# Selective-scan block on one core: the scan's input u*B moved to TensorE, the readout over four blocks, the squares and a quarter of the weighing by C on VectorE

## The chip, the cores and the metric

The kernel runs on 1 core of one Trainium2 chip. The metric is the device time of one execution in microseconds. Times below come from 3 runs and from one more execution that the hardware profiler recorded.

## The reference, cut to what matters

x has 2 sequences of 2048 steps and 256 channels. A feed-forward block, the selective-scan block and the feed-forward block again are applied, each with its residual. The change is about the scan:

```python
dt = soft_clamp(softplus(xc @ W_dt.T + b_dt), 0.001, 0.1, 0.5)     # [2, 2048, 512]
Bp = xc @ W_B.T;  Cp = xc @ W_C.T                                  # [2, 2048, 16]
dA = exp(soft_clamp(dt[..., None] * A, -8.0, 8.0, 0.5))            # [2, 2048, 512, 16]
dB = dt[..., None] * Bp[:, :, None, :]
def step(h, inp):                                                  # h: [2, 512, 16]
    h = h * dA_t + dB_t * x_t[:, :, None]
    nrm = sqrt(sum(h * h, axis=(1, 2)))
    fac = minimum(20.0 / (nrm + 1e-08), 1.0)
    h = where(t % 10 == 0, h * fac, h)
    y = einsum('bdn,bn->bd', h, C_t) + D_param * x_t
    return h, y
```

Every tenth step the state of a sequence is rescaled by its norm over all 512 x 16 entries, so blocks of ten steps have to follow each other.

## The kernel before, in words

The kernel has three stages, each written out by hand as one instruction list per engine, with semaphores between them: pre_stage (first feed-forward block, projections, convolution, dt and u = dt*xc; 8 tiles of 256 steps), scan_stage and post_stage (output projection and second feed-forward block). Between stages the tensors go through DRAM.

In the scan stage the 512 channels are 4 groups (KE) of 128 partitions. A *unit* m is one block j = m // 2 of ten steps of one sequence b = m % 2: there are NB = 205 blocks and UNITS = 410 units. A unit holds 64 rows (4 groups x 16 states, NCH) of 11 columns (W): column 0 takes the state that is carried over, the other ten the steps. Per unit the engines do this (lines of the profile in brackets):

- ScalarE: two rows of tanh for a later chunk (L924, `tanhs`), the copy of a sum out of PSUM (L942, `copy_q`), the decays by exp (L952), the carry, which writes the rescaled last state of unit m - 2 into column 0 of unit m in PSUM (L960), and the squares of the last state with their sum per partition (L934, `squares`).
- VectorE: `inputs`, the product u*B of the unit after next, written to PSUM (L1031), and `scan`, the recurrence itself over 704 columns, decays from SBUF and inputs from PSUM (L1042). u lies in PSUM: TensorE copies six blocks of it there at a time with an identity product (L856, `move_u`); only the last half chunk is read from SBUF.
- TensorE: the sum over partitions of the squares (L850, `total`), the readout, which sums the weighted states over the 16 states n by accumulating identity products over a pair of blocks (L867), and `repeat`, one readout product done once more into a place that nothing reads (L877).
- POOL: `norm`, which clips the sum (L813) and takes its power -1/2 (L818), and `weigh`, the product of the 640 states with C into hc (L826). Its list is norm(m + 2), weigh(m), norm(m + 3), weigh(m + 1) and so on.
- SP issues the loads. C and B come as blocks broadcast over the partitions (`load_bc`), u as half chunks.

A float32 product on TensorE is two records in the trace. The squares of unit m + 2 wait for the scan of m, the sum for the squares, the copy for the sum, `norm` for the copy, the carry for `norm`, and the scan of m + 2 for the carry: the loop that passes from scan to scan of one sequence, with the other sequence in between.

```python
            scan(m)
            if m + B < UNITS:
                inputs(m + B)
```

Of the kernel before, what the change touches and what calls it, by code (L numbers as in the profile page):

```python
# [13 lines left out]
P = 128  # L14
B, L, D = 2, 2048, 256
E = 512
# [17 lines left out]
HALF = CT // 2  # L34
# [9 lines left out]
SECOND = 96 * 1024  # L44
# [4 lines left out]
    zT_ready yT_ready v_place""")  # L49


def pre_stage(nc, dram, w, areas, banks, sem):
# [28 lines left out]
    v_place = second.offset  # L81
    v = second.put("v", [P, KE, COLS])
    e = second.put("e", [P, KE, COLS])
# [13 lines left out]
    raw2 = e[:].rearrange("p a (c d) -> p (a c) d", d=D)  # L97
# [48 lines left out]
    def dt_u(dve, i):  # L146
# [3 lines left out]
        dve.tensor_scalar(dt[:], e[:], DT_HALF / SHARP, DT_MID, ALU.mult, ALU.add).then_inc(dt_ready, 1)  # L150
# [5 lines left out]
    def sync(sp, scan, post):  # L156
# [39 lines left out]
        sp.dma_start(dram["bc"][:, :, L:LP], zero[0:2 * N, 0:B, :]).then_inc(padded, 16)  # L196
        store_r(0)
        for i in range(TILES):
# [8 lines left out]
            if i >= 1:  # L207
                store_dt_u(sp, i - 1)
            if i < LAST:
                store_r(i + 1)  # L210
            if i == 3:
                post.load_params(sp)
                sp.wait_ge(padded, 48)
                scan.load_first(sp)
        store_bc(LAST)

    def gpsimd(pool):
# [42 lines left out]
    def tensor(pe):  # L260
# [24 lines left out]
        def down(i):  # L285
            if i >= 1:
                pe.wait_ge(yT_ready, KD * i)
            for d in range(KD):
# [58 lines left out]
        for i in range(TILES):  # L347
# [16 lines left out]
            project_dt(i, 1, KE)  # L364
        project_bc(LAST)

    def scalar(act, scan, post):
# [54 lines left out]
        def softplus(i, m0, m1):  # L422
            if i >= 1:
                act.wait_ge(th_ready, i)
# [4 lines left out]
        def tanh_v(i):  # L429
            act.wait_ge(ring_read, use["dt", i, KE - 1] + 1)  # L430
            if i >= 1:
                act.wait_ge(dt_ready, i)
            act.activation(e[:], v[:], ACT.Tanh, scale=SHARP / (DT_HALF + 1e-8),
# [30 lines left out]
        for i in range(TILES):  # L464
            copy_z(i)
            if i == LAST:
                scan.tanhs(act, 0, 8, 14)
            if i >= 1:
# [37 lines left out]
        scan.squares(act, 0)  # L506
        scan.squares(act, 1)
# [8 lines left out]
    def vector(dve, scan, post):  # L516
# [102 lines left out]
        dve.wait_ge(padded, 48)  # L619
        for i in range(TILES):  # L620
            if i + 2 < TILES:
                stats1(i + 2)
                apply1(i + 2)
            convolve(i)
# [10 lines left out]
            if i == 4:  # L635
                scan.decay_scale(dve)
                post.residual_steps(dve)
# [3 lines left out]
               t3_done, conv_steps, xc_ready, zT_ready, yT_ready, v_place)  # L641
# [4 lines left out]
PAIRS = -(-NB // 2)  # L646
NCH = KE * N
HB = CB // 2
HALVES = -(-NB // HB)
# [6 lines left out]
DRING = 6  # L656

Scan = namedtuple("Scan", """sync gpsimd tensor scalar vector load_first tanhs decay_rates decay_scale
    decay_ready y_out y_copied y_summed inp_ready squares copy_q""")
# [14 lines left out]

def scan_stage(nc, dram, w, areas, banks, sem, pre):

# [866 lines left out]
```

## Time and profile before

| what | us |
|---|---|
| median of 3 runs (lowest, highest) | 1652.79 (1650.85, 1653.66) |
| profiled execution, its own time | 1652.22 |
| its span, first to last instruction | 1650.4 |
| VectorE busy | 1387.6 (84%) |
| TensorE busy (products) | 1382.1 (84%) |
| ScalarE busy | 1268.5 (77%) |
| POOL busy | 978.3 (59%) |
| mean granted clock of TensorE | 0.991 |

The pre stage fills roughly the first 425 us, the scan 425 to 1440 us, the post stage the rest. Busy shares are of the whole span; a stage has its own. A duration in the timeline runs from an instruction's start to its end, and since neighbours on an engine overlap a little, the step from one start to the next can be shorter than the duration.

### The profile page before, as it was taken

What the parts mean: (1) busy time and instruction counts of PE and PEld (TensorE: products, weight loads), DVE (VectorE), ACT (ScalarE), POOL (GpSimd) and SP (SyncE); (2) the same over time, 40 slices, a digit from 0 to 9 for tenths busy, and PEclk for the clock granted to TensorE, in tenths of its full rate; (3) what the DMA queues carried; (4) which work ended last, traced back from release to release, by engine and by line L of the source; (5) the groups of instructions that cost most, each with busy time, mean ns of one, the idle gap of its engine ahead of it and who ended that gap; (6) DMA issues with size and microseconds to landing.
All of it is one profiled execution on the core that took longest, in us unless ns stands there. A gap on an engine that the chain in (4) does not pass through costs nothing.

```text
span 1650.4 us, 24684 instructions
## 1 busy us (share of the span) xinstructions
PE 1382.1 (84%) x7160; PEld 1055.6 (64%) x7160; DVE 1387.6 (84%) x1684; ACT 1268.5 (77%) x3354; POOL 978.3 (59%) x1318
## 2 busy tenths in 40 slices
PE   6999999999577787778777777777777877799998
PEld 5555555553366666666666666666666666677776
DVE  7757655645599999999999999999999999987885
ACT  4454455558899999999999999999999996433333
POOL 1302222112388888988888888888888888800000
PEclk9999999999799999999999999999999999999999
DMA  7223356224244333433433342434243235565430
GB/s 244 77 78 97 111 148 165 76 92 143 73 122 112 84 93 91 105 80 102 108 86 93 92 105 75 109 85 105 77 113 83 79 89 160 154 205 160 147 115 26
DMA packets 202694, 179.88 MB, mean 109 GB/s; under 512 B 82816, under 2 KB 175040, under 8 KB 202560
## 3 DMA queue, kind: packets, MB, share of 16 engines
q1 hardware_dynamic: 201616, 176.99, 38.7%
q8 instruction: 58, 0.95, 0.2%
q10 hardware_dynamic: 944, 1.31, 0.2%
q14 instruction: 76, 0.62, 0.1%
HBM read 125.26 MB, written 53.57 MB: 108 GB/s over the span
## 4 chain that ended last, share of the span: by engine, by line
DVE 44%; PE 29%; issue 17%; ACT 6%; POOL 3%; DMA 1%; DVEq 0%; ACTq 0%; SPq 0%; POOLq 0%
DVE h L1042 35%; PE banks L326 7%; PE banks L318 5%; PE banks L293 4%; ACT tb L924 3%; PE banks L1185 3%; PE banks L1206 3%; DVE cv L585 3%; PE banks L1216 2%; DVE banks L1031 2%; PE banks L333 2%; POOL hc L826 1%; PE banks L867 1%; ACT sc_sq L934 1%; PE banks L281 1%
## 5 line engine op out<-in xcount | busy, mean ns | idle before, releaser
L1042 DVE TENSOR_TENSOR_SCAN h<-decay,banks 128x704 f32<-128x704 f32 x410 | 660.2, 1610 | 9.7 <-ACT banks L960 9.2
L867 PE MATMUL banks<-hc,w_ident 128*128 128x160 f32 (+1 forms) x3296 | 611.9, 309 | 18.2 <-POOL hc L826 17.7
L826 POOL TENSOR_TENSOR hc<-h,bc 128x640 f32<-128x640 f32 x410 | 590.8, 1441 | 0.0
L867 PEld LDWEIGHTS banks<-hc,w_ident 128*128 128x128 f32 x3296 | 485.5, 191 | 38.8 <-POOL hc L826 29.9
L924 ACT ACTIVATE tb<-dtc,a 128x320 f32<-128x320 f32 (+1 forms) x832 | 448.8, 556 | 4.8 <-DVE x L552 4.8
L1031 DVE TENSOR_TENSOR banks<-banks,bc 128x640 f32<-128x640 f32 x408 | 339.6, 833 | 44.4 <-issue 14.5
L850 PE MATMUL banks<-sc_ss,sc_ones 128*128 128x1 f32 x820 | 156.0, 259 | 215.3 <-ACT sc_sq L934 207.5
L850 PEld LDWEIGHTS banks<-sc_ss,sc_ones 128*128 128x128 f32 x820 | 123.2, 189 | 307.4 <-ACT sc_sq L934 303.3
L952 ACT ACTIVATE decay<-tb 128x640 f32<-128x640 f32 x410 | 298.1, 728 | 0.4
L818 POOL TENSOR_TENSOR rc<-qs,w_mhalf 128x1 f32<-128x1 f32 x410 | 226.8, 553 | 61.7 <-POOL qs L813 1.3
L236 POOL TENSOR_TENSOR ln_rz<-ln_vz,w_mhalf 128x4 f32<-128x4 f32 x8 | 13.9, 1734 | 280.8 <-DVE ln_vz L558 280.8
L877 PE MATMUL banks<-hc,w_ident 128*128 128x160 f32 x800 | 174.2, 299 | 0.0
L960 ACT ACTIVATE banks<-h,rc 128x64 f32<-128x64 f32 x410 | 154.2, 376 | 21.3 <-POOL rc L818 21.3
L813 POOL TENSOR_SCALAR qs<-nq 128x1 f32<-128x1 f32 x410 | 79.5, 194 | 114.3 <-ACT nq L942 84.2
L877 PEld LDWEIGHTS banks<-hc,w_ident 128*128 128x128 f32 x800 | 130.6, 190 | 0.0
L934 ACT ACTIVATE sc_sq<-h 128x64 f32<-128x64 f32 x410 | 125.4, 306 | 5.5 <-DVE h L1042 4.7
L318 PE MATMUL banks<-zT,win 128*128 128x512 f32 x256 | 113.8, 598 | 6.8 <-ACT gf L383 5.8
L326 PE MATMUL banks<-xc,wdt 128*128 128x512 f32 x256 | 114.1, 600 | 3.1 <-ACT sg L420 3.1
L1172 POOL TENSOR_TENSOR q_ln_rs<-q_ln_ve,w_mhalf 128x4 f32<-128x4 f32 x8 | 10.9, 1366 | 167.3 <-DVE q_ln_ve L1443 167.3
L1273 ACT ACTIVATE q_gf<-banks,w_b,w_a 128x512 f32<-128x512 f32 x64 | 50.0, 781 | 69.4 <-PE banks L1206 65.6
L318 PEld LDWEIGHTS banks<-zT,win 128*128 128x128 f32 x256 | 47.4, 190 | 68.5 <-issue 59.9
L942 ACT ACTIVATE nq<-banks 128x1 f32<-128x1 f32 x410 | 68.8, 168 | 24.5 <-PE banks L850 22.3
(109 smaller groups left out, 1621.0 us busy)
## 6 DMA issues: line engine op xcount, KB each, us to landing
bc<-scratch_blk SPq DMA_DIRECT2D x205, 320.0 KB, 3.5
uc<-scratch_u SPq DMA_DIRECT2D x35, 240.0 KB, 4.5
scratch_xc<-xc SPq DMA_DIRECT2D x8, 1024.0 KB, 4.8
scratch_sg<-sg SPq DMA_DIRECT2D x8, 1024.0 KB, 5.9
scratch_dt<-dt SPq DMA_DIRECT2D x8, 1024.0 KB, 6.2
scratch_u<-u SPq DMA_DIRECT2D x8, 1024.0 KB, 6.9
q_ys<-scratch_y SPq DMA_DIRECT2D x8, 1024.0 KB, 6.0
q_xc<-scratch_xc SPq DMA_DIRECT2D x8, 1024.0 KB, 8.8
```

Source lines behind the costliest of these rows:

```text
L318: mm = pe.matmul(out, win[:, k, (m0 + m) * P:(m0 + m + 1) * P], zT[:, k, :], start=(k == 0), stop=(k == KD - 1))
L326: mm = pe.matmul(out, wdt[:, k, m * P:(m + 1) * P], xc[:, i % 2, k, :], start=(k == 0), stop=(k == KE - 1))
L818: pool.tensor_tensor(rc[:, b:b + 1], qs[:, b:b + 1], w.mhalf[:, 0:1], ALU.pow).then_inc(norm_ready, 1)
L826: pool.tensor_tensor(hc[:, pl % 2, :, j % 2 * S:(j % 2 + 1) * S] .rearrange("p (c b n) e -> p c b n e", c=KE, b=B)[:, :, b], state(m)[:, : ...
L850: pe.matmul(psQ[:, b:b + 1], ones[:], ss[:, b:b + 1], start=True, stop=True).then_inc(sum_ready, 1)
L867: mm = pe.matmul(psY[:, 0:KE * B * wide], w.ident[:], rhs, start=(n == 0), stop=(n == N - 1))
L877: pe.matmul(psQ[:, P:P + KE * B * 2 * S], w.ident[:], rhs, start=True, stop=True)
L924: act.activation(tanh_rows(c, r), dtc[:, c % 2, k * B:(k + 1) * B, 0:blocks_of(c) * S].rearrange("p b (k e) -> p k b e", e=S), ACT.Tanh, s ...
L952: act.activation(decay[:, m % DRING].rearrange("p (g i e) -> p g i e", g=DB, e=W)[:, :, :, 1:], tanh_block(j, b), ACT.Exp, scale=DTA_HALF ...
L960: act.activation(inp(m)[:, :, 0], state(m - B)[:, :, S], ACT.Copy, scale=rc[:, b:b + 1]).then_inc(carry_ready, 1)
L1031: dve.tensor_tensor(inp(m)[:, :, 1:].rearrange("p (c n) e -> p c n e", c=KE), u[:, b, :, o:o + S].unsqueeze(2).broadcast_to([P, KE, N, S]) ...
L1042: dve.tensor_tensor_scan(state(m).rearrange("p r e -> p (r e)"), decay[:, m % DRING], psI[m % B][:, 0:NCH * W], 0.0, ALU.mult, ALU.add).th ...
```

## The change

u*B is no longer made on VectorE. For every unit TensorE makes it as four float32r products (`inputs`, L988 of the changed kernel), one for each group of channels: the stationary operand holds u of the ten steps, each as high and low part and twice, in 40 rows; the moving operand holds B of these steps at the columns of their own step, 176 wide, zero elsewhere. The sum over the 40 rows gives u*B in float32r parts, and zero in column 0. The two operands are prepared in 32 *pieces* of 128 steps: load, transposes on TensorE (`turn_piece`), high part on ScalarE (`high_piece`), low part on VectorE (`low_piece`), the spreading of B by a mask on POOL (`mask_piece`), and the store to DRAM (`store_piece`). Pieces 0 and 1 are made within the pre stage, behind tiles 4 and 5; pieces 2 to 31 within the loop, one each 12 units. SP loads one unit's 40 rows per unit (`load_unit`), four units ahead.

The squares go from ScalarE to VectorE, behind the scan. The fourth group of channels of the weighing by C goes from POOL to VectorE (`weigh_last`), behind the squares. The readout takes four blocks at once (320 columns), a quad, in place of two (160 columns); `move_u` and `repeat` go. In the pre stage the buffer e goes (tanh works in place), and VectorE makes the masks once, behind tile 4.

```diff
         def weigh(m):
             j, b = m // B, m % B
-            pl = j // 2
+            pl = j // QB
+            if b == 0:
+                pool.wait_ge(bc_in[j % RING], 16 * (j // RING + 1))
             pool.wait_ge(h_ready, m + B + 1)
...
+            place, states, weights = weighed(m, 0, KE - 1)
+            pool.tensor_tensor(place, states, weights, ALU.mult).then_inc(hc_ready, 1)
...
+        def inputs(m):
+            pe.wait_ge(ub_in[m % URING], 16 * (m // URING + 1))
+            if m >= B:
+                pe.wait_ge(h_ready, m + 1)
+            for c in range(KE):
+                mm = pe.matmul(psI[m % B][:, c * N * W:(c + 1) * N * W], ub[m % URING][:, c * P:(c + 1) * P],
+                               ub[m % URING][:, E:], start=True, stop=True)
+            mm.then_inc(inp_ready, 1)
...
-                readout(p, quarter * 4, quarter * 4 + 3)
-                if m < UNITS - 6:
-                    repeat(p, m + B)
-                readout(p, quarter * 4 + 3, quarter * 4 + 4)
+                readout(p, part * each, (part + 1) * each)
...
-            if m + B < UNITS:
-                squares(act, m + B)
...
+        def squares(m):
+            b = m % B
+            dve.wait_ge(h_ready, m + 1)
             if m >= B:
-                dve.wait_ge(h_ready, m + 1)
-            dve.tensor_tensor(
-                inp(m)[:, :, 1:].rearrange("p (c n) e -> p c n e", c=KE),
-                u[:, b, :, o:o + S].unsqueeze(2).broadcast_to([P, KE, N, S]),
-                bc[j % RING][:, 0, b].unsqueeze(1).broadcast_to([P, KE, N, S]),
-                ALU.mult).then_inc(inp_ready, 1)
+                dve.wait_ge(sum_ready, m - B + 1)
+            last = state(m - B)[:, :, S]
+            dve.scalar_tensor_tensor(out=sq[:, b, :], in0=last, scalar=1.0, in1=last, op0=ALU.mult, op1=ALU.mult,
+                                     accum_out=ss[:, b:b + 1]).then_inc(sq_ready, 1)
...
+        def weigh_last(m):
...
+            place, states, weights = weighed(m, KE - 1, KE)
+            dve.wait_ge(h_ready, m + B + 1)
+            dve.tensor_tensor(place, states, weights, ALU.mult).then_inc(last_ready, 1)
...
         for m in range(UNITS):
             scan(m)
             if m + B < UNITS:
-                inputs(m + B)
+                squares(m + B)
+            weigh_last(m)
+            if m - 1 in pieces:
+                low_piece(dve, pieces[m - 1], psT)
...
+            if i in (4, 5):
+                scan.load_piece(sp, i - 4)
+            if i in (5, 6):
+                scan.store_piece(sp, i - 5)
```

`weighed(m, c0, c1)` gives the places in hc, the states in h and the values of C (tile bc) for the groups c0 to c1 of a unit. h, hc, bc and sc_sq lie in SBUF.

How the instructions stand on VectorE in the middle of the loop, before (h<-decay,banks is the scan, banks<-banks,bc the product u*B; banks are PSUM):

```order
L1042 SCALAR_TENSOR_TENSOR h<-decay,banks 128x704 [waits hc_ready,decay_ready,carry_ready]
L1031 TENSOR_TENSOR banks<-banks,bc_101 128x64x10 [waits h_ready]
L1042 SCALAR_TENSOR_TENSOR h<-decay,banks 128x704 [waits hc_ready,decay_ready,carry_ready]
L1031 TENSOR_TENSOR banks<-banks,bc_102 128x64x10 [waits h_ready,bc_in3]
L1042 SCALAR_TENSOR_TENSOR h<-decay,banks 128x704 [waits hc_ready,decay_ready,carry_ready]
```

and on VectorE in the changed kernel, at the same place, with one piece in it:

```order
L1158 SCALAR_TENSOR_TENSOR h<-decay,banks 128x704 [waits hc_ready,last_ready,decay_ready,carry_ready]
L1149 SCALAR_TENSOR_TENSOR sc_sq,sc_ss<-h 128x64 [waits sum_ready,h_ready]
L1170 TENSOR_TENSOR hc<-h,bc_97 128x16x10 [waits h_ready,bc_in1]
L1158 SCALAR_TENSOR_TENSOR h<-decay,banks 128x704 [waits hc_ready,last_ready,decay_ready,carry_ready]
L1149 SCALAR_TENSOR_TENSOR sc_sq,sc_ss<-h 128x64 [waits sum_ready,h_ready]
L1170 TENSOR_TENSOR hc<-h,bc_97 128x16x10 [waits h_ready]
L853 TENSOR_TENSOR turned<-banks,turned 128x528 [waits ut_hi]
```

Two short instructions with h as an input have taken the product's place. POOL in the changed kernel, with qs and rc the two operations of `norm`, and the same piece:

```order
L959 TENSOR_TENSOR hc<-h,bc_96 128x3x16x10 [waits h_ready]
L943 TENSOR_SCALAR qs<-nq 128x1 [waits q_copied]
L948 TENSOR_TENSOR rc<-qs,w_mhalf 128x1 [waits q_held,carry_ready]
L959 TENSOR_TENSOR hc<-h,bc_97 128x3x16x10 [waits h_ready,bc_in1]
L943 TENSOR_SCALAR qs<-nq 128x1 [waits q_copied]
L948 TENSOR_TENSOR rc<-qs,w_mhalf 128x1 [waits q_held,carry_ready]
L959 TENSOR_TENSOR hc<-h,bc_97 128x3x16x10 [waits h_ready]
L861 TENSOR_TENSOR spread<-turned,mask 128x352 [waits ub_out,ut_lo]
```

Its order is the old one; the weighing is three groups wide in place of four. On TensorE, before:

```order
L850 MATMUL banks<-sc_ss,sc_ones 128x1 [waits q_copied,sq_ready]
L867 MATMUL banks<-hc,w_ident 128x160 x3
L877 MATMUL banks<-hc,w_ident 128x160 [waits q_copied]
L867 MATMUL banks<-hc,w_ident 128x160
L850 MATMUL banks<-sc_ss,sc_ones 128x1 [waits q_copied,sq_ready]
```

and in the changed kernel:

```order
L981 MATMUL banks<-sc_ss,sc_ones 128x1 [waits q_copied,sq_ready]
L988 MATMUL banks<-ub_101 128x176 [waits h_ready,ub_in1]
L988 MATMUL banks<-ub_101 128x176 x3
L1001 MATMUL banks<-hc,w_ident 128x320 x2
L981 MATMUL banks<-sc_ss,sc_ones 128x1 [waits q_copied,sq_ready]
```

The sum still leads the unit; the four input products stand between it and the readout, which is two products of double width.

## Rows read from the trace of the kernel before

**Rows 1.** Stretches: start:end, us, PE PEld DVE ACT POOL busy (x), PEclk, DMA share, GB/s.

```profile
500.00:900.00 400.00, 316.41 (x2000) 271.59 (x2001) 386.87 (x329) 393.82 (x1193) 352.64 (x495) 1.00 0.38 96
900.00:1300.00 400.00, 316.56 (x2003) 271.50 (x2002) 386.83 (x330) 394.17 (x1193) 352.96 (x494) 1.00 0.37 93
```

**Rows 2.** Groups by line and form, VectorE, whole span: busy us, mean ns.

```profile
L1031 DVE TENSOR_TENSOR banks<-banks,bc 128x640 f32<-128x640 f32 x408 | 339.6, 833 | 44.4 <-issue 14.5 <-DVE h L1042 0.9
...
L585 DVE SCALAR_TENSOR_TENSOR cv<-xbuf,convw,cv 128x512 f32<-128x512 f32 x96 | 65.0, 747 | 0.0
...
L1053 DVE TENSOR_TENSOR h<-u,b 128x64 f32<-128x64 f32 x2 | 0.4, 276 | 0.0
```

**Rows 3.** Timeline of one unit, all engines: start us, us, instruction.

```profile
901.35 1.06 PE L867 MATMUL banks<-hc,w_ident 128*128 128x160 f32 x6
...
901.81 0.19 POOL L813 TENSOR_SCALAR qs<-nq 128x1 f32<-128x1 f32 x1
...
902.15 0.55 POOL L818 TENSOR_TENSOR rc<-qs,w_mhalf 128x1 f32<-128x1 f32 x1
...
902.66 1.45 POOL L826 TENSOR_TENSOR hc<-h,bc 128x640 f32<-128x640 f32 x1
902.71 0.83 DVE L1031 TENSOR_TENSOR banks<-banks,bc 128x640 f32<-128x640 f32 x1
902.73 0.38 ACT L960 ACTIVATE banks<-h,rc 128x64 f32<-128x64 f32 x1
...
903.25 0.18 ACT L934 ACTIVATION_READ_ACCUMULATOR sc_sq<-h 128x1 f32 x1
...
903.45 1.61 DVE L1042 TENSOR_TENSOR_SCAN h<-decay,banks 128x704 f32<-128x704 f32 x1
...
903.49 0.38 PE L850 MATMUL banks<-sc_ss,sc_ones 128*128 128x1 f32 x2 [0.54 <-ACT sc_sq L934]
...
903.91 0.17 ACT L942 ACTIVATE nq<-banks 128x1 f32<-128x1 f32 x1
...
904.20 0.19 POOL L813 TENSOR_SCALAR qs<-nq 128x1 f32<-128x1 f32 x1
```

**Rows 4.** Timeline, end of the loop, POOL and VectorE.

```profile
1433.81 1.44 POOL L826 TENSOR_TENSOR hc<-h,bc 128x640 f32<-128x640 f32 x1
...
1434.30 1.64 DVE L1031 TENSOR_TENSOR banks<-uc,bc 128x640 f32<-128x640 f32 x1
...
1435.34 0.64 POOL L813 TENSOR_SCALAR qs<-nq 128x1 f32<-128x1 f32 x1
...
1438.69 1.61 DVE L1042 TENSOR_TENSOR_SCAN h<-decay,banks 128x704 f32<-128x704 f32 x1
```

**Rows 5.** Timeline, 24 us earlier, POOL and VectorE.

```profile
1405.78 1.44 POOL L826 TENSOR_TENSOR hc<-h,bc 128x640 f32<-128x640 f32 x1
...
1406.99 0.79 DVE L1303 SCALAR_TENSOR_TENSOR q_ys<-q_xc,dpar,q_ys 128x512 f32<-128x512 f32 x1
```

**Rows 6.** Timeline of VectorE: scans of units 0, 10 and 392.

```profile
429.76 1.61 DVE L1042 TENSOR_TENSOR_SCAN h<-decay,banks 128x704 f32<-128x704 f32 x1
...
460.86 1.62 DVE L1042 TENSOR_TENSOR_SCAN h<-decay,banks 128x704 f32<-128x704 f32 x1 [0.35 <-ACT banks L960]
...
1392.60 1.61 DVE L1042 TENSOR_TENSOR_SCAN h<-decay,banks 128x704 f32<-128x704 f32 x1
```

**Rows 7.** Busy time by stretch, start of the loop; columns as in rows 1.

```profile
440.00:445.00 5.00, 0.59 (x2) 0.50 (x2) 3.94 (x5) 4.79 (x14) 3.94 (x6) 0.50 0.18 66
455.00:460.00 5.00, 3.48 (x24) 3.24 (x24) 4.40 (x4) 4.99 (x17) 3.67 (x7) 1.00 1.07 326
```

**Rows 8.** Timeline at the end of tile 4 of the pre stage: SP, TensorE.

```profile
278.75 0.51 SPq L137 DMA_DIRECT2D scratch_u<-u  x1
...
282.01 1.04 PE L311 MATMUL banks<-w_ident,zn 128*128 128x128 f32 x8
```

**Rows 9.** The page, DMA issues: KB each, median us from issue to landing.

```profile
uc<-scratch_u SPq DMA_DIRECT2D x35, 240.0 KB, 4.5
```

More of the change, by code:

```diff
@@ L258, in gpsimd, with tensor @@
                 norm2(i + 1)
-    def tensor(pe):
+            if i in (5, 6):
+                scan.mask_piece(pool, i - 5)
+    def tensor(pe, scan):
         def fill(what):
@@ L636, in vector @@
                 scan.decay_scale(dve)
+                scan.masks(dve)
                 post.residual_steps(dve)
@@ L656 @@
 DRING = 6
[L658 to L659 removed]
+URING = 4
+PIECES = B * L // P
+SPLITS = 4
+ROW = E + N * W
+Scan = namedtuple("Scan", """sync gpsimd tensor scalar vector load_first load_units tanhs decay_rates decay_scale masks
+    decay_ready y_out y_copied copy_q load_piece turn_piece high_piece low_piece mask_piece store_piece ut_lo""")
 def chunk_of(j):
@@ new lines, in store_piece @@
+    def store_piece(sp, k):
+        t, b = k // B * P, k % B
+        rows = dram["ub"][b, t:t + P].rearrange("t (r h) x -> t r h x", h=2)
+        sp.wait_ge(ut_lo, k + 1)
+        for r in range(2):
+            sp.dma_start(rows[:, r, :, 0:E], turned[:, :, 0:E].bitcast(F32)).then_inc(ub_out, 16)
+        sp.wait_ge(spread_done, k + 1)
+        for half in range(2):
+            sp.dma_start(rows[:, :, half, E:], spread[:].bitcast(F32).rearrange("p r n e -> p r (n e)")
+                         ).then_inc(ub_out, 16)
@@ L870, in readout @@
                 mm.then_inc(y_summed, 1)
-        def repeat(p, m):
-            pe.wait_ge(q_copied, m + 1)
-            rhs = hc[:, p % 2].rearrange("p (c n) t -> p c n t", n=N)[:, :, 0]
-            pe.matmul(psQ[:, P:P + KE * B * 2 * S], w.ident[:], rhs, start=True, stop=True)
+        pieces = {piece_unit(k): k for k in range(B, PIECES)}
+        each = N // (QB * B)
         pe.wait_ge(consts, 1)
+        pe.wait_ge(pre.zT_ready, KD * TILES)
+        pe.wait_ge(pre.yT_ready, KD * TILES)
+        pe.wait_ge(ut_lo, B)
+        inputs(0)
+        inputs(1)
         pe.wait_ge(pre.ring_read, len(pre.order))
-        total(0)
-        move_u(0)
-        total(1)
+        for m in range(B):
+            total(m)
         for m in range(UNITS):
@@ L988, in rows_at @@
             return c + 1, half
+        pieces = {piece_unit(k): k for k in range(B, PIECES)}
         for m in range(AHEAD):
@@ L1057, in vector @@
                 ALU.mult).then_inc(h_ready, 1)
+        for m in range(B):
+            squares(m)
         dve.wait_ge(zeroed, 1)
-        for m in range(B):
-            inputs(m)
         pre.dt_u(dve, TILES - 1)
+        dve.wait_ge(pre.ring_read, len(pre.order))
+        dve.wait_ge(pre.sg_out, 16 * TILES)
+        dve.wait_ge(pre.xc_out[0], 16 * TILES // 2)
+        dve.wait_ge(pre.u_ready, TILES)
+        pieces = {piece_unit(k): k for k in range(B, PIECES)}
         for m in range(UNITS):
@@ L1236, in tensor @@
         turn_xn(0)
[L1237 removed]
+        pe.wait_ge(scan.y_copied, QUADS)
         up(0, 0, 1)
@@ L1490, in _ @@
             def _(pe):
-                pre.tensor(pe)
+                pre.tensor(pe, scan)
                 scan.tensor(pe, post)
```

294 lines of the change are left out of this document (183 added, 111 removed).

## The prediction

> **What bounds the kernel now.** The busy table puts VectorE, TensorE and ScalarE all near 80% of the span, which says only that several engines are close. The stretches tell more [rows 1]: from 500 to 1300 us VectorE is busy for 97% and ScalarE for 98% of the time, and two VectorE operations are counted per unit (one batch's ten steps), so 659 operations in 800 us make 2.43 us a unit. The by-form groups and the timeline say what fills a unit: the scan takes 1.61 us and its successor starts some 1.7 us after it, and the product u*B takes 0.833 us with the next scan 0.74 us behind its start [rows 2, 3]. VectorE waits for nothing; 1.7 + 0.74 is the period.
>
> Beside it runs a loop that comes back every second unit: squares, the sum on TensorE, its copy on ScalarE, two small POOL operations (L813, L818), the carry, the scan. On POOL the weighing by C (L826) stands behind those two and is 1.44 us long [rows 3]. Today nothing on VectorE cares when the weighing runs.
>
> The third reading is the one that decides. At the end of the loop u comes from SBUF and not from PSUM, and the same product with two SBUF inputs takes 1.64 us where it took 0.83 [rows 4]. It starts at 1434.30, while POOL's weighing runs from 1433.81 to 1435.25, and ends at 1435.94, 0.69 us after the weighing. That is 640 elements at one per 1.04 ns and almost nothing else: VectorE got no element through while POOL's instruction ran. The scalar_tensor_tensor of 512 elements does the same: weighing over at 1407.22, product over at 1407.78, 0.56 us later [rows 5]. It works the other way as well: the short L813, 0.19 us elsewhere, starts at 1435.34 and lasts until 1435.98, just past the end of VectorE's product [rows 3, 4]. So on this chip a VectorE instruction with both inputs in SBUF and a POOL instruction that reads SBUF exclude each other for their whole length. The scan and the old product read one input from PSUM and aren't stretched: the one at 902.71 lies beside a weighing from 902.66 and takes 0.83 us, the mean of all 408 [rows 2, 3].
>
> **The change, part by part.**
>
> *Per unit on VectorE.* The product (0.74 us of step) goes. The squares come, 64 elements through scalar_tensor_tensor with both inputs the same SBUF column, and a quarter of the weighing, 160 elements of h by C, both in SBUF. From the 512-element row of 0.747 us, at 1.04 ns an element, the fixed part is 0.21 and the squares 0.28 us [rows 2]; the step to the next operation is about 0.09 less, as with the product. Writing the accumulator is not in the trace for VectorE. ScalarE's costs 0.09 us of step [rows 3]; bounds are 0 and the 0.18 us of its whole length, and I take 0.10. The quarter weighing is between 0.28 (64 elements) and 0.83 us (640 elements), by its size 0.32, step 0.24. Without any exclusion a unit would be 1.68 + 0.20 + 0.10 + 0.24 = 2.22 us, 0.22 under today's.
>
> The Trainium skill (VectorE: DVE Perf Modes, the section on the TRN2 errata) gives an fp32 tensor_tensor as element count plus 151 cycles at 0.96 GHz, which would make 64 elements 0.224 us. The row here shows 0.276 for 64 elements [rows 2], so the measured one is used; by the page that sum would be 2.17.
>
> *Per unit on POOL.* The weighing falls to 480 elements: 1441 x 3/4 = 1.08 us, or 1.13 if 0.19 us of it is fixed (the shortest POOL row). I take 1.08.
>
> *The order that follows.* POOL's queue is L813, L818, weighing; the first two wait for the squares of the same pass. I follow one pass from the moment the previous weighing frees SBUF: squares through 0.09 (64 elements and the 0.02 seen at 1434.30), accumulator 0.10, to TensorE 0.06 (903.43 to 903.49), TensorE to the copy 0.42, copy to L813 0.29, L813 to L818 0.34, L818 to the weighing 0.51, the weighing itself 1.08 [rows 3]. That makes 2.89 us. Meanwhile VectorE does squares 0.19, quarter weighing 0.25, scan 1.65 and comes to the next squares at 2.1. The weighing has been running since 1.81. So the squares wait 0.8 us, every unit, and what they wait for is itself started by the squares before: a closed ring of **2.89 us** a unit. The carry is in at 1.30 + 0.58 + 0.4 = 2.3, before its scan is wanted at 3.3, so it adds nothing. The wait is new; behind it on VectorE stand the quarter weighing and the scan, and TensorE, ScalarE and POOL wait in turn.
>
> *The other engines fit beneath it.* ScalarE loses squares and accumulator (0.30) of 2.43, leaving about 2.1. TensorE: the readout issues 4 records of 320 columns in place of 8 of 160, at 0.15 a 160-column record (six in 1.06 us, the last of which runs 0.3) [rows 3] 1.2 us at most; ten records become four, since the repeated products go too; four input products of 176 columns at no more than 0.15 each 0.6; the sum 0.24. That is 2.0, hidden under 2.89; without that cover it would still be under 2.22. Loads of C halve, the 410 loads of u and B rows stand on SP, four units ahead: nothing waits on them.
>
> *The 30 pieces within the loop* put five transposes on TensorE, 528 elements each on ScalarE and VectorE (0.69 us for 512 from PSUM, 0.62 of step) and 352 elements on POOL (0.8 us at the weighing's rate). VectorE has 0.8 us free and POOL about 0.9 between weighing and L813, so I count 0; if each cost its POOL time in full it would be 24 us.
>
> *Before the loop.* SP issues the store of u at 278.75 in tile 4, the piece load follows behind it and lands some 4.5 us after issue, at about 284; TensorE is at the place of the transposes at 282 [rows 8, 9] and TensorE is what runs through there. Two pieces, each 2 to 3 us of wait and 0.7 of transposing, and some of the masks' 5 us on VectorE that isn't hidden: +8 (0 to 15). The two products ahead of the first scan go: -1.5.
>
> *Sum.* The first ten units take 3.11 us each now (429.76 to 460.86), since ScalarE has extra rows to do; at 2.89 that is -2. From 460.86 to 1392.60 lie 382 units at 2.44 [rows 6]: 382 x 0.45 = +172. The last sixteen take 2.88 us already, with skip and gate between (1392.60 to 1438.69) [rows 4, 6]; their two-SBUF operations will meet POOL more often: +2. Together -1.5 - 2 + 172 + 2 + 8 = +178. The profiled execution took 1652.2 us (span 1650.4 and 1.8 around it), the median of the runs is 1652.8, the same within 0.04%. 1652.2 + 178 = **1830 us**.
>
> **The rivals.**
>
> *Squares and weighing miss each other (faster).* The ring closes only because the weighing starts (1.81) before the scan ends (2.1): 0.3 us decides. If the squares, having one tensor as both inputs, took only one SBUF read, or such small instructions slipped in, VectorE would set 2.22 us: 382 x -0.22 = -84, the pieces then cost VectorE's 0.62 each, +19, before the loop +8, start and end -7: **1588 us**. Against it: both directions of the exclusion stand in the trace for tensor_tensor and for scalar_tensor_tensor. Also, squares ahead of the weighing don't help much: the quarter weighing right behind would then be the one shut out, with the scan behind it. For it: no row has an instruction this short, nor twice the same input. The Trainium skill (SBUF — State Buffer, Who interferes with whom) has the rule that speaks against this change: VectorE instructions with two SBUF inputs contend with POOL instructions that read SBUF, and the one that starts second is blocked fully. By that rule the squares are no exception; the trace agrees where it can be read (0.95 us of blocking at 1434.30). Chance 0.16.
>
> *They queue without the chain adding to it.* If POOL's work and VectorE's two short ones stood end to end, with no wait for the sum in between, a unit would be 0.34 + 0.51 + 1.08 + 0.10 (from the weighing's end to the next L813) + 0.19 + 0.25 = 2.47: 1671 us; orders that change from unit to unit lie between 2.47 and 2.89, to 1760 or so. It needs the weighing to be late often. 0.09, of which 0.03 ends within 0.2% of no change.
>
> *TensorE's clock falls.* The repeated products go, and TensorE's columns per unit with them. The granted clock stood at 0.50 (1.2 GHz) while TensorE did one sum per 3 us, and at 1.00 (2.4 GHz) from 455 on with ten records in 2.8 us [rows 7]; afterwards there are 4 x 320 + 4 x 176 columns in 2.89 us, more than 10 x 160 in 2.8. At half clock the readout alone is 2.3 us and the unit about 3.5: +405, **2060 us**. The Trainium skill (TensorE: Matmul & The Clock Gate, "A second HAM failure mode") reports a kernel in which brief idle spells between groups of products let the clock swing; no row here shows that inside the loop. 0.03.
>
> **How the numbers follow.** Forecast 0.72, missing each other 0.16, partly queued 0.09, clock 0.03. High end: weighing 1.13, accumulator 0.19 give 3.03 a unit, +225, and pieces at their full 24 with 8 before the loop: 1910. Low end: 1690, which takes in most of the partly queued orders and leaves out the fast case. Of no change this kernel's measurement can tell about 0.2%. Faster 0.16, same 0.03, slower 0.81.
>
> **What would show it.** Right: scans 2.89 us apart; the squares' row with a mean near 0.95 us where 0.28 is their own length, each ending just behind a weighing; the quarter weighing unstretched at 0.32; the weighing at 1.08; ScalarE's and TensorE's idle time on the squares' chain; clock 1.00. Wrong: squares at 0.3 us while the weighing runs (first rival), or scan steps over 3.2 with the clock at 0.50 (third).

## The result, and the profile after

The changed kernel takes 1830.87 us (median of 4 runs, 1828.37 to 1831.7) where the kernel before takes 1652.32 in the same comparison: ratio 1.1078, 95% interval 1.1059 to 1.1097. The forecast was 1830, with 1690 to 1910 as its range. The profiled execution has a span of 1826.5 us, 176.1 more than before.

Stretches of the loop, in the columns of [rows 1]:

```profile
500.00:900.00 400.00, 295.30 (x1456) 199.89 (x1455) 392.96 (x575) 299.85 (x731) 265.81 (x433) 0.98 0.48 134
900.00:1300.00 400.00, 299.57 (x1467) 203.83 (x1468) 392.70 (x576) 300.23 (x733) 265.51 (x434) 0.97 0.47 132
```

VectorE counts as busy for 98% of the time, TensorE, ScalarE and POOL for less than before. Someone with only this view would say that VectorE got too much work. The groups of the page say otherwise:

```profile
L1158 DVE TENSOR_TENSOR_SCAN h<-decay,banks 128x704 f32<-128x704 f32 x410 | 659.3, 1608 | 10.4 <-ACT banks L1084 7.4
...
L959 POOL TENSOR_TENSOR hc<-h,bc 128x480 f32<-128x480 f32 x410 | 461.4, 1125 | 1.0 <-DVE h L1158 0.6
...
L981 PE MATMUL banks<-sc_ss,sc_ones 128*128 128x1 f32 x820 | 158.4, 262 | 309.0 <-DVE sc_sq L1149 306.5
...
L1149 DVE SCALAR_TENSOR_TENSOR sc_sq<-h 128x64 f32<-128x64 f32 x410 | 368.0, 898 | 14.2
...
L943 POOL TENSOR_SCALAR qs<-nq 128x1 f32<-128x1 f32 x410 | 78.5, 191 | 375.7 <-ACT nq L1066 373.1
...
L1170 DVE TENSOR_TENSOR hc<-h,bc 128x160 f32<-128x160 f32 x410 | 152.5, 372 | 3.1 <-issue 1.8
```

64 elements of squares take 898 ns on average, while 160 elements of the quarter weighing take 372. The profile counts the time for which an instruction is blocked as busy time; it shows in the mean of one, set against its size. The idle time of TensorE (306.5 us) and POOL (373.1 us) stands on the chain that the squares start.

One unit in the timeline (start, us, instruction), against [rows 3]:

```profile
1000.31 0.17 ACT L1066 ACTIVATE nq<-banks 128x1 f32<-128x1 f32 x1 [0.80 <-PE banks L981]
...
1000.57 0.19 POOL L943 TENSOR_SCALAR qs<-nq 128x1 f32<-128x1 f32 x1 [0.87 <-ACT nq L1066]
...
1000.90 0.55 POOL L948 TENSOR_TENSOR rc<-qs,w_mhalf 128x1 f32<-128x1 f32 x1
1001.42 1.12 POOL L959 TENSOR_TENSOR hc<-h,bc 128x480 f32<-128x480 f32 x1
...
1001.63 1.03 DVE L1149 SCALAR_TENSOR_TENSOR sc_sq<-h 128x64 f32<-128x64 f32 x1
...
1002.60 0.08 DVE L1149 DVE_READ_ACCUMULATOR sc_sq<-h 128x1 f32 x1
1002.60 0.32 DVE L1170 TENSOR_TENSOR hc<-h,bc 128x160 f32<-128x160 f32 x1
...
1002.73 0.38 PE L981 MATMUL banks<-sc_ss,sc_ones 128*128 128x1 f32 x2 [0.83 <-DVE sc_sq L1149]
1002.84 1.61 DVE L1158 TENSOR_TENSOR_SCAN h<-decay,banks 128x704 f32<-128x704 f32 x1
...
1003.15 0.17 ACT L1066 ACTIVATE nq<-banks 128x1 f32<-128x1 f32 x1 [0.80 <-PE banks L981]
```

The squares start 0.21 us behind the weighing's start and end 0.12 us after its end at 1002.54. So it is in 322 units: where squares start within a weighing and last over 0.6 us, they end 0.11 to 0.14 us behind it. The ring comes round in 2.84 us (1000.31 to 1003.15): squares 0.12 behind the weighing, sum 0.07, copy 0.42, qs 0.26, rc 0.33, weighing 0.52, its length 1.12.

Where the 176 us lie, by the starts of scans (of after here, of before in [rows 6] and the last scan at 1440.20):

| stretch | before | after | difference | forecast |
|---|---|---|---|---|
| to the first scan | 429.8 | 442.6 | +12.8 | +6.5 |
| first ten units | 31.1 | 30.2 | -0.9 | -2 |
| 382 units in the middle | 931.7 | 1090.1 | +158.3 | +172 |
| the last 17 steps | 47.6 | 48.95 | +1.4 | +2 |
| behind the last scan's start | 210.2 | 214.7 | +4.5 | 0 |

```profile
442.57 1.62 DVE L1158 TENSOR_TENSOR_SCAN h<-decay,banks 128x704 f32<-128x704 f32 x1 [2.88 <-ACT decay L1076]
...
1611.81 1.62 DVE L1158 TENSOR_TENSOR_SCAN h<-decay,banks 128x704 f32<-128x704 f32 x1
```

### The profile page after: what moved, and what is told of

Its sections match the earlier page's. It is cut to its first block, busy times and chain, and to the rows that moved or that the text cites. A ratio compares the mean times of both kernels' runs of the same rounds, so it can differ in the third digit from the quotient of the medians.

```text
span 1826.5 us, 25399 instructions
## 1 busy us (share of the span) xinstructions
PE 1472.9 (81%) x6460; PEld 976.7 (53%) x6460; DVE 1565.1 (86%) x2553; ACT 1159.3 (63%) x2515; POOL 871.8 (48%) x1350
## 4 chain that ended last, share of the span: by engine, by line
PE 35%; POOL 35%; DVE 12%; issue 8%; ACT 6%; DMA 2%; POOLq 1%; SPq 0%; DVEq 0%; ACTq 0%
POOL hc L959 21%; POOL rc L948 10%; PE banks L981 8%; PE banks L330 4%; PE banks L338 4%; POOL qs L943 4%; ACT nq L1066 3%; PE banks L305 3%; PE banks L1322 3%; PE banks L1001 3%; PE banks L1343 3%; DVE cv L597 3%; DVE h L1158 2%; DVE sc_sq L1149 2%; PE banks L1353 2%
## 5 line engine op out<-in xcount | busy, mean ns | idle before, releaser
L1001 PE MATMUL banks<-hc,w_ident 128*128 128x320 f32 (+1 forms) x1664 | 537.3, 448 | 0.8 <-ACT yc L1095 0.6
L959 POOL TENSOR_TENSOR hc<-h,bc 128x480 f32<-128x480 f32 x410 | 461.4, 1125 | 1.0 <-DVE h L1158 0.6
L981 PE MATMUL banks<-sc_ss,sc_ones 128*128 128x1 f32 x820 | 158.4, 262 | 309.0 <-DVE sc_sq L1149 306.5
L981 PEld LDWEIGHTS banks<-sc_ss,sc_ones 128*128 128x128 f32 x820 | 128.9, 195 | 509.3 <-DVE sc_sq L1149 504.0
L1149 DVE SCALAR_TENSOR_TENSOR sc_sq<-h 128x64 f32<-128x64 f32 x410 | 368.0, 898 | 14.2
L1001 PEld LDWEIGHTS banks<-hc,w_ident 128*128 128x128 f32 x1664 | 290.1, 195 | 71.7 <-issue 6.0
L988 PE MATMUL banks<-ub 128*128 128x176 f32 x1640 | 282.3, 296 | 2.5 <-DMA ub<-scratch_ub 2.5
L943 POOL TENSOR_SCALAR qs<-nq 128x1 f32<-128x1 f32 x410 | 78.5, 191 | 375.7 <-ACT nq L1066 373.1
L988 PEld LDWEIGHTS banks<-ub 128*128 128x128 f32 x1640 | 226.1, 200 | 3.4 <-DMA ub<-scratch_ub 2.6
L1170 DVE TENSOR_TENSOR hc<-h,bc 128x160 f32<-128x160 f32 x410 | 152.5, 372 | 3.1 <-issue 1.8
```

The costliest lines, as they stand in the source:

```text
L959: pool.tensor_tensor(place, states, weights, ALU.mult).then_inc(hc_ready, 1)
L981: pe.matmul(psQ[:, b:b + 1], ones[:], ss[:, b:b + 1], start=True, stop=True).then_inc(sum_ready, 1)
L988: mm = pe.matmul(psI[m % B][:, c * N * W:(c + 1) * N * W], ub[m % URING][:, c * P:(c + 1) * P], ub[m % URING][:, E:], start=True, stop=True)
L1001: mm = pe.matmul(psY[:, 0:KE * B * wide], w.ident[:], rhs, start=(n == 0), stop=(n == N - 1))
L1149: dve.scalar_tensor_tensor(out=sq[:, b, :], in0=last, scalar=1.0, in1=last, op0=ALU.mult, op1=ALU.mult, accum_out=ss[:, b:b + 1]).then_inc ...
```

## The experiments

Ratios are to the kernel before, with 95% intervals. Each edit is to the changed kernel unless it says otherwise. "Median unit" is the median step from scan to scan in the middle of the loop.

### Who shuts out whom

**Squares with one input from PSUM**

```diff
-            dve.scalar_tensor_tensor(out=sq[:, b, :], in0=last, scalar=1.0, in1=last, op0=ALU.mult, op1=ALU.mult,
+            other = last if m < B else inp(m - B)[:, :, S]
+            dve.scalar_tensor_tensor(out=sq[:, b, :], in0=last, scalar=1.0, in1=other, op0=ALU.mult, op1=ALU.mult,
```

> The squares read one input from SBUF and the other from PSUM (the last column of the unit's u*B), so the norm is computed of other numbers. Ring theory: squares and POOL's weighing no longer exclude each other, squares fall from 0.90 us mean to about 0.28 and don't wait; the quarter weighing behind them still has two SBUF inputs and now meets the weighing instead, stretched to 0.6 to 0.7 us. Unit about 2.5 us, whole kernel 1650 to 1730 us. Rival (the squares instruction is slow by itself, strided reading and an accumulator): squares stay near 0.9 us, 1830 us.

1678.42 us, 1.0148 (1.0118 to 1.0177). Its groups:

```profile
L1171 DVE TENSOR_TENSOR hc<-h,bc 128x160 f32<-128x160 f32 x410 | 255.3, 623 | 2.9 <-PE banks L1001 1.2 <-issue 0.4
...
L1150 DVE SCALAR_TENSOR_TENSOR sc_sq<-h,banks 128x64 f32<-128x64 f32 x408 | 108.9, 267 | 14.1
```

The same operation of the same size fell from 898 to 267 ns because one input moved to PSUM, and the time fell by 152 us. The quarter weighing, still with two SBUF inputs, was then the one that was stretched, 372 to 623 ns; but no sum waits for it, so the ring is gone and the median unit is 2.41.

**Both short instructions with one input from PSUM**

```diff
+                pe.wait_ge(last_ready, m - B + 1)
...
+            other = last if m < B else inp(m - B)[:, :, S]
...
+            weights = inp(m)[:, (KE - 1) * N:, 1:].rearrange("p (c n) e -> p c n e", c=1)
```

> Squares and the quarter weighing both take their second input from PSUM (other numbers than the reference's; TensorE's next products into that bank wait for the quarter weighing). Ring theory: nothing on VectorE meets POOL any more, VectorE sets the unit at 1.65 + 0.34 + 0.24 = 2.25 us plus 0.6 per piece, about 2.3: whole kernel 1590 to 1625 us. Rival (short instructions slow by themselves): 1830 us. Rival (TensorE with half clock spells and readout sets the pace): 2.4 us a unit or more, 1650 us or more.

1598.61 us, 0.9665 (0.9601 to 0.973). In its timeline both run right beside the weighing:

```profile
1000.23 1.12 POOL L959 TENSOR_TENSOR hc<-h,bc 128x480 f32<-128x480 f32 x1
1000.30 0.27 DVE L1151 SCALAR_TENSOR_TENSOR sc_sq<-h,banks 128x64 f32<-128x64 f32 x1
1000.49 0.08 DVE L1151 DVE_READ_ACCUMULATOR sc_sq<-h,banks 128x1 f32 x1
1000.49 0.32 DVE L1173 TENSOR_TENSOR hc<-h,banks 128x160 f32<-128x160 f32 x1
...
1000.72 1.61 DVE L1160 TENSOR_TENSOR_SCAN h<-decay,banks 128x704 f32<-128x704 f32 x1
```

With the exclusion gone and the same instructions left on every engine, the time is 3.4% under the kernel before. It is a measurement and no kernel to use, since the squares and the quarter take numbers that are not theirs. The whole loss is the exclusion, then. The median unit is 2.08; the rival in the prediction had 2.22, since it gave the accumulator read 0.10 of step (it starts together with the next instruction: none) and the scan 1.68 (1.65).

**Squares back on ScalarE, the quarter weighing on VectorE**

```diff
+        act.activation(sq[:, b, :], state(m - B)[:, :, S], ACT.Square,
+                       accum_out=ss[:, b:b + 1]).then_inc(sq_ready, 1)
...
-            if m + B < UNITS:
-                squares(m + B)
             weigh_last(m)
```

> Squares back on ScalarE, quarter weighing left on VectorE. Ring theory: the sum no longer waits for the weighing; the quarter weighing meets the weighing and holds the scan up, unit about 2.5 us (ScalarE's own work 2.35), 1660 to 1730 us. Rival (slow squares instruction): the quarter weighing stays at 0.32, unit 2.35 by ScalarE, about 1640 us.

1707.25 us, 1.0322 (1.0292 to 1.0352), median unit 2.36, the quarter weighing at 612 ns. Where the quarter weighing gets ahead of POOL's it takes 0.33 us; elsewhere it is shut out, and the scan behind it with it. The period stays under the ring's, as in the first run: what is shut out starts no sum.

### Is it the 0.3 us?

**The whole weighing on POOL, squares on VectorE**

```diff
-            place, states, weights = weighed(m, 0, KE - 1)
+            place, states, weights = weighed(m, 0, KE)
...
-            weigh_last(m)
```

> POOL does the whole weighing again (640 columns), VectorE no quarter. VectorE's own work falls by 0.24 us a unit. Ring theory: the weighing is a link of the ring and VectorE's work is not, so the unit grows by 1.44 - 1.12 = 0.32 to 3.16 us, +128 us: 1940 to 1965 us. Rival (VectorE bound by slow short instructions): 0.24 less a unit, about 1735 us.

1706.21 us, 1.0316 (1.0286 to 1.0346). No theory had this. A weighing a third longer was to lengthen the ring; instead the squares are shut out in 47 units of 410:

```profile
1000.23 0.27 DVE L1147 SCALAR_TENSOR_TENSOR sc_sq<-h 128x64 f32<-128x64 f32 x1
...
1000.48 1.45 POOL L958 TENSOR_TENSOR hc<-h,bc 128x640 f32<-128x640 f32 x1
...
1002.87 1.44 POOL L958 TENSOR_TENSOR hc<-h,bc 128x640 f32<-128x640 f32 x1
...
1003.19 1.24 DVE L1147 SCALAR_TENSOR_TENSOR sc_sq<-h 128x64 f32<-128x64 f32 x1
...
1006.01 0.27 DVE L1147 SCALAR_TENSOR_TENSOR sc_sq<-h 128x64 f32<-128x64 f32 x1
1006.02 1.57 POOL L958 TENSOR_TENSOR hc<-h,bc 128x640 f32<-128x640 f32 x1
```

At 1000.23 the squares start 0.25 us before the weighing, and the unit takes 2.38 us (2.39 from weighing to weighing: POOL's own 0.34, 0.52 and 1.53). At 1003.19 a unit of the ring follows, and the next one leaves it. That weighing ends at 1004.31; 1.71 us later the next weighing starts, as in the changed kernel (1.72, by the rows above), but the squares are there after 1.70 us and not after 1.93, since no quarter weighing stands before the scan. They win by 0.01 us and take 0.27. The same happens behind every such unit between 485 and 1440 us: the next squares start 0.01 to 0.06 us ahead of the weighing, which then takes 1.53 to 1.57 us in place of 1.44. So the 0.24 us of the quarter weighing on VectorE are what keeps the ring closed in the changed kernel. The prediction saw that some 0.3 us decide it, but not that a quarter of the weighing is what closes it. (No run takes away the quarter and leaves POOL's weighing at 480 elements; the 1.71 us do not depend on its length.)

**The quarter of C in PSUM too, nothing else moved** (with the early loads from below)

```diff
+            pe.matmul(copied(m), w.ident[:], bc[m // B % RING][:, m % B].rearrange("p n e -> p (n e)"),
+                      start=True, stop=True)
...
             place, states, weights = weighed(m, KE - 1, KE)
+            weights = copied(m).rearrange("p (c n e) -> p c n e", c=1, n=N)
```

> The changed kernel with early loads of the two pieces, and the quarter of C copied to PSUM by TensorE (one more product of 160 columns a unit), so that the quarter weighing reads one input from PSUM. POOL's order has no wait added. Ring theory: only the squares have to be shut out for the ring to close, since the scan still ends about 0.24 us later through the quarter weighing than without it; squares stay near 0.9 to 1.0 us, the unit at 2.8 to 2.85, 1815 to 1830 us. Rival: the quarter must be shut out too for the loop to stay in that order; then the unit goes to about 2.35 and the time to 1680 to 1700 us, like the whole weighing on POOL.

1820.09 us, 1.1011 (1.0994 to 1.1027), against 1819.79 with the early loads alone. The squares take 958 ns on average, the quarter weighing 310, the unit 2.84. With only the squares shut out the ring stays closed: whether the quarter is shut out plays no part. That its 0.24 us of VectorE's time do, the rows of the run before say.

### Changing the order on POOL

**The weighing waits for VectorE's next squares**

```diff
             pool.wait_ge(h_ready, m + B + 1)
+            pool.wait_ge(sq_ready, min(m + B + 2, UNITS))
```

> The changed kernel with one more wait: POOL starts the weighing of unit m only when the squares of unit m + 3 (the next ones on VectorE) are through. Nothing is computed otherwise. Ring theory: the squares can no longer be shut out, and the sum is on its way before the weighing runs. What is open is who gets SBUF next. If the quarter weighing, which VectorE issues at once behind the squares, comes before POOL has seen the semaphore: unit 2.4 us or so (half of 1.65 + 0.35 squares + 0.25 + 1.13 weighing + 0.34 + 0.58 + 0.43), 1650 to 1710 us. If the weighing comes first, as the prediction on record says of squares that lead: the quarter weighing and the scan wait, 3.2 us and more, 1970 us. Rival (slow squares instruction): a wait more can only cost, 1830 us or above.

1699.02 us, 1.0278 (1.0258 to 1.0299). One added wait takes 132 us off: the squares at 278 ns, the quarter weighing at 323 without being shut out. It starts right behind the squares, and the weighing 0.23 us or more behind its start (1006.52 and 1006.75). Now the short units take 2.1 to 2.55, but each piece in the loop makes some of 3.4 to 3.6.

**The POOL wait, with the quarter of C in PSUM**

> As x11_squares_first, and C for the quarter weighing is copied into PSUM by TensorE (an identity product of 160 columns per unit beside the four input products), so that the quarter weighing has one SBUF input. Computes what the reference asks. Ring theory: neither short instruction is ever shut out, unit between VectorE's 2.25 and the chain's 2.3 us, TensorE 2.3: 1595 to 1640 us, under both kernels. Rival (TensorE's 0.3 us more make it the bound, with its clock falling): 2.5 us and more, 1690 us or above.

1693.52 us, 1.0245 (1.0228 to 1.0262): 5 us better and no more. There was no stretching left to remove (316 ns against 323). The forecast put the remaining loss on the quarter; it lay with the pieces. Their low part waits for ScalarE's high part with the scan queued behind it:

```profile
1004.50 0.71 DVE L856 TENSOR_TENSOR turned<-banks,turned 128x528 fp32r<-128x528 f32 x1 [0.81 <-ACT turned L852]
...
1005.12 1.61 DVE L1167 TENSOR_TENSOR_SCAN h<-decay,banks 128x704 f32<-128x704 f32 x1
```

**The weighing ahead of the norm**

```diff
-            pool.wait_ge(h_ready, m + B + 1)
+            pool.wait_ge(last_ready, m + 1)
...
+            weigh(m)
             if m + B < UNITS:
                 norm(m + B)
-            weigh(m)
```

> POOL's list is turned: the weighing of unit m directly behind VectorE's quarter of the same unit, and then the two norm operations. Ring theory: the weighing never stands before the squares, but it now stands before the norm and lengthens the loop through the carry: (1.65 + 0.35 + 0.25 + 1.13 + 0.1 + 0.34 + 0.58 + 0.43) / 2 = 2.4 us, 1660 to 1700 us. Rival (slow squares instruction): the longer loop shows and the squares stay at 0.9 us, 1830 us or above.

1711.74 us, 1.0355 (1.0334 to 1.0376). Nothing is stretched (squares 271 ns, quarter 321); most units alternate between 2.08 and 2.78. The norm now waits for the weighing (qs 0.09 us behind its end), and every second scan waits 0.6 to 0.8 us for the carry.

**Only the inputs on TensorE: squares on ScalarE, the whole weighing on POOL**

> Only the other two parts of the change: inputs as float32r products on TensorE with their pieces, readout over four blocks; squares on ScalarE, whole weighing on POOL, so VectorE has no instruction with two SBUF inputs in the loop but the scan alone. Ring theory: POOL's own 0.34 + 0.51 + 1.54 = 2.39 us sets the unit and the pieces cost POOL 0.9 each (27 us): 1650 to 1690 us. It says what the first two parts are worth alone, against 1654 before.

1707.18 us, 1.0327 (1.0307 to 1.0348), above the 1650 to 1690 expected. (The scan reads one of its inputs from PSUM, so no VectorE instruction in this loop has two SBUF inputs.) The plain unit is 2.38, POOL's own time, against 2.44 before, and the units with a piece go to 3.5 and more; the first scan is at 448.07 against 429.76. Taking the product off VectorE gains next to nothing per unit once POOL's full weighing is the bound at nearly the same period, and the pieces and the later start cost more than that.

### The 12.8 us before the loop, and the pieces

**Loads of pieces 0 and 1 issued earlier**

```diff
         for i in range(TILES):
+            if i == 5:
+                scan.load_piece(sp, 1)
...
-            if i in (4, 5):
-                scan.load_piece(sp, i - 4)
+            if i == 3:
+                scan.load_piece(sp, 0)
```

> The changed kernel, with the loads of pieces 0 and 1 issued earlier on SP's queue: the first straight behind the store of u that it waits for, the second at the head of the following tile. Nothing in the loop is touched. If the 12.8 us by which the first scan comes later are TensorE's two waits for those loads (6.2 and 5.5 us in the chain of waits), the first scan comes 8 to 11 us earlier and the whole is 1820 to 1823 us. If the delay is the transposes, the copies and the masks themselves, the time stays at 1829 to 1831.

1819.79 us, 1.1009 (1.0993 to 1.1025), 11.1 us less. The first scan comes at 431.37 and not 442.57. In the changed kernel the chain of waits had these two links, which are gone:

```profile
280.98 6.21 DMA piece_b<-scratch_bc
...
338.91 5.46 DMA piece_b<-scratch_bc
```

A link counts from the load's issue. TensorE itself had nothing to do for 4.48 and 3.71 us ahead of the transposes, 8.2 us in all:

```profile
287.24 1.12 PE L841 MATMUL banks<-w_ident,piece 128*128 128x128 f32 x4 [4.48 <-DMA piece_b<-scratch_bc]
...
288.53 1.97 PE L323 MATMUL banks<-w_ident,zn 128*128 128x128 f32 x8
...
344.41 1.11 PE L841 MATMUL banks<-w_ident,piece 128*128 128x128 f32 x4 [3.71 <-DMA piece_b<-scratch_bc]
```

The other 3 us go with its clock. After the first wait the granted clock is 0.50 from 287.2 to 293 us; with the early loads it is 1.00 from 280 to 300. The same products take 0.60 and not 1.12 us (the four transposes) and 1.09 and not 1.97 (the eight behind them).

```profile
282.60 0.60 PE L843 MATMUL banks<-w_ident,piece 128*128 128x128 f32 x4
...
283.30 1.09 PE L325 MATMUL banks<-w_ident,zn 128*128 128x128 f32 x8
```

In the runs that keep the late loads the first scan lies anywhere from 442.57 (the changed kernel) to 448.61 us; what makes it differ is not known.

**The POOL wait, early loads, and the parts of a piece spread over more units**

```diff
-            if m - 1 in pieces:
-                mask_piece(pool, pieces[m - 1])
+            if m - 3 in pieces:
+                mask_piece(pool, pieces[m - 3])
...
-            if m - 1 in pieces:
-                low_piece(dve, pieces[m - 1], psT)
+            if m - 2 in pieces:
+                low_piece(dve, pieces[m - 2], psT)
```

> As the kernel in which POOL's weighing waits for the squares of the unit after next (1699 us), with the early loads of the first two pieces, and the parts of the 30 pieces in the loop spread over three units more evenly: low part one unit later on VectorE, mask two units later on POOL. The early loads give 8 to 10 us. If the pieces cost because their parts fall one after another into the same turn of the loop, spreading gives back 0.5 to 1 us of each, 15 to 30 us: 1660 to 1675 us. If each part costs its own length wherever it stands, only the loads' gain is left: 1689 to 1691.

1652.67 us, 0.9999 (0.999 to 1.0009): the time of the kernel before, better than expected. Its page and timeline:

```profile
L1161 DVE TENSOR_TENSOR_SCAN h<-decay,banks 128x704 f32<-128x704 f32 x410 | 663.2, 1618 | 96.2 <-ACT banks L1087 90.3
...
L962 POOL TENSOR_TENSOR hc<-h,bc 128x480 f32<-128x480 f32 x410 | 467.8, 1141 | 99.7 <-DVE sc_sq L1152 87.5
...
L1152 DVE SCALAR_TENSOR_TENSOR sc_sq<-h 128x64 f32<-128x64 f32 x410 | 111.3, 272 | 14.0
```

```profile
1000.95 0.27 DVE L1152 SCALAR_TENSOR_TENSOR sc_sq<-h 128x64 f32<-128x64 f32 x1
1001.15 0.08 DVE L1152 DVE_READ_ACCUMULATOR sc_sq<-h 128x1 f32 x1
1001.15 0.32 DVE L1173 TENSOR_TENSOR hc<-h,bc 128x160 f32<-128x160 f32 x1
...
1001.40 1.13 POOL L962 TENSOR_TENSOR hc<-h,bc 128x480 f32<-128x480 f32 x1 [0.26 <-DVE sc_sq L1152]
```

The weighing now follows squares and quarter. From the first scan (431.24) to the last (1433.73) it is 1002.5 us, where the kernel with the POOL wait alone takes 1036.0: 33.5 us for 30 pieces, 1.1 us each. The rest of the 46 us comes from the first scan, at 431.24 in place of 447.34. The kernel before takes 1010.4 from first scan to last. In the profiled executions the loop is 8 us faster than before, then, and the rest of the program gives 6 back. One wait of the loop stands out: TensorE waits 4.45 us for a load of u and B rows near the start.

```profile
465.78 1.15 PE L991 MATMUL banks<-ub 128*128 128x176 f32 x4 [4.45 <-DMA ub<-scratch_ub]
```

**All of it with the quarter of C in PSUM**

> The same with the quarter of C copied to PSUM by TensorE, so that the quarter weighing reads one input from PSUM (1693.5 us without early loads and without spreading). Spreading matters: 8 to 10 us from the loads and 15 to 30 from the pieces, 1655 to 1670 us, which is still not under the kernel before. It does not: 1684 to 1686.

1659.43 us, 1.0041 (1.0028 to 1.0054). 7 us slower than without the copy: VectorE idles 13 us ahead of the quarter weighing for TensorE's readout, which the added product makes later. Only the kernel with both inputs exchanged, which computes other numbers, is faster than the kernel before.

## Why the prediction was right

**The ring** (the order that follows). Right in mechanism, place and nearly in size: 2.89 forecast, 2.84 measured, mean step 2.85 with the pieces in it. The terms: the squares come through 0.12 behind the weighing (0.09 forecast); the accumulator with the way to TensorE takes 0.07, not 0.16; the weighing takes 1.12, not 1.08 (1441 ns for 640 elements and 1125 for 480 leave a fixed part of 0.18 us, which the sum had left out and the high bound had at 0.19). Each is small, and 382 units make 13.7 us of them, although the mean lies some 5 us in all above 382 plain units. The squares' mean is 898 ns (forecast near 950) and the quarter's 372 (0.32, mean over a few shut out). In a unit of the ring the squares take 1.03 us; the prediction's own terms give 0.89 (2.98 less 2.09), since it had VectorE reach them 0.16 us later.

**That the total is right within 1 us is partly luck.** The middle of the loop came out 13.7 us under its term and the last steps 0.6 under; the start was 6.3 over, the tail 4.5 and the first ten units 1.1. Together that is 2.4 under.

**The exclusion** was inferred from three instructions at the end of the loop [rows 4, 5]. It holds for a 64-element scalar_tensor_tensor with one tensor as both inputs, on which the first rival had set its hope. The PSUM experiment shows the cause, not only the coincidence: 267 ns with PSUM as the second input, a median of 1028 without. With both inputs in SBUF the same instruction takes 271 to 279 ns in the runs whose order on POOL keeps the weighing away from it, so neither its reading pattern nor its accumulator is what is slow. The Trainium skill (SBUF — State Buffer, Who interferes with whom) says that the one that starts second is blocked fully; the trace agrees, with 0.12 us from POOL's end to the squares' end in a unit where they start 0.91 us before that end. For POOL's short rc operation the rows at the end of this document show no such blocking, although it reads SBUF too; there the measurement decides.

**The margin.** The weighing starts before the scan ends by 0.2 us (1001.42 against 1001.60), 0.3 by the prediction. The whole-weighing run shows that taking 0.24 us of work off VectorE is enough to lose it.

**Wrong: "squares ahead of the weighing don't help much: the quarter weighing would be the one shut out".** With the wait on the squares POOL starts 0.25 us behind the quarter weighing (1001.15 and 1001.40 above), which runs at 323 ns, and 132 us are gained. The step reckoned with POOL's queue as it was; here the squares' semaphore reached POOL later than VectorE's own next instruction started. This one wait turns the forecast loss into 2.8%.

**Before the loop**, +12.8 for +6.5: the term mis-sized is the wait for the piece loads, 4.48 and 3.71 us of TensorE rather than 2 to 3 each, and the clock behind the waits had no term at all (some 3 of the 11.2 us that the early loads give back). The load was taken to land 4.5 us after issue, at 284, with TensorE arriving at 282; but its second half was issued only at 280.98 and took 6.2 us by itself. With the loads early the first scan is 1.6 us later than before: that is the transposes, copies and masks, less the two products that are gone.

**The tail**, +4.5 for 0, was not in the sum. The last whole quad is read out behind the last scan as 28 products of 320 columns, which TensorE does ahead of the second feed-forward block's transposes; before it was 24 of 160. First after, then before:

```profile
1615.84 7.70 PE L1001 MATMUL banks<-hc,w_ident 128*128 128x320 f32 x28
```

```profile
1444.78 3.42 PE L867 MATMUL banks<-hc,w_ident 128*128 128x160 f32 x24
```

**Pieces in the loop**, 0 forecast and next to 0 found: steps of 3.46, 2.82 and 2.26 us around one sum to 8.54, three plain ones to 8.52. That holds under the ring, whose waits are the cover. In the kernel with the POOL wait they are gone, and spreading a piece's parts gives back 1.1 us of each.

**The clock** did not decide. It stood at 0.50 (1.2 GHz) for longer than before [rows 7]:

```profile
450.00:460.00 10.00, 5.84 (x23) 4.92 (x23) 9.73 (x15) 8.74 (x23) 7.15 (x12) 0.50 0.30 81
460.00:470.00 10.00, 5.12 (x20) 4.44 (x20) 9.89 (x16) 7.94 (x20) 5.76 (x10) 0.50 0.71 231
```

Four units there take 3.05 us rather than 2.84, about 1 us in all. The seven steps from 475.67 to 499.25 take 3.7 us more than seven plain ones: in the first TensorE waits 2.51 us for a load of u and B rows, and the clock is 0.67 from 470 to 480 and 0.81 from 480 to 500; no run separates the two. From 500 to 1300 us it is 0.97 to 0.98 and not the 1.00 of the prediction, with the plain unit at 2.84.

**The price of the quarter weighing.** The row 316 to 323 ns agrees with what the Trainium skill states for tensor_tensor (VectorE: DVE Perf Modes, TRN2 errata), 324 ns for 160 elements. The squares, a scalar_tensor_tensor of 64 elements, take 267 ns, above the 224 that the rule gives for a tensor_tensor of that size, as the 64-element row did in the prediction.

What stays open: why the kernel with the whole weighing falls back into the ring for single units (26 of 35 such squares between 485 and 1440 us start 2.27 us behind a piece's low part, the other 9 do not), and whether the 6 us outside the loop and the one wait for a load could be had back; neither was tried.

## What to carry to other kernels

A short VectorE instruction with two SBUF inputs that starts within a long POOL instruction waits for its end: here squares of 0.27 us ended 0.11 to 0.14 us behind a weighing of 1.12. Put one input into PSUM, or let POOL wait for the short one. Ask first whether the POOL instruction itself depends, by any chain, on the one that it shuts out: then the wait closes into a ring and is paid every time. A share of busy time (98% here) cannot show this: compare the mean of one instruction with its size.

Work that is free under a wait has a price once the wait is gone: here the 30 pieces, whose spreading was worth 33 us in the loop with the POOL wait. In the changed loop, where three steps around a piece sum to 8.54 us against 8.52, there is nothing for it to give back; no run tried it.

## What was not expected of the hardware

The kernel with the whole weighing on POOL has two rhythms, plain units of 2.38 us and single ones of the ring, and the changed kernel stays in the ring at 2.84; a margin of 0.2 us between two queues decided 125 us (1830.87 against 1706.21). The accumulator read of VectorE (78 ns) starts together with the next instruction (both at 1002.60 above) and costs it no step, where the prediction read 0.09 us for ScalarE's [rows 3]. The rc operation (L818 before, 0.55 us) does not shut out VectorE: in the run with the POOL wait the squares start inside it and take their plain 0.27 us.

```profile
1003.68 0.55 POOL L948 TENSOR_TENSOR rc<-qs,w_mhalf 128x1 f32<-128x1 f32 x1
1003.78 0.27 DVE L1150 SCALAR_TENSOR_TENSOR sc_sq<-h 128x64 f32<-128x64 f32 x1
```
